# Four chained attention layers on one core: cross attention's first group of heads worked pair by pair

## What is computed

```python
def _mha(qx, kx, wq, bq, wk, bk, wv, bv, wo, bo, mask, bias):
    ...
    s = jnp.einsum('bhqd,bhkd->bhqk', q, k) / jnp.sqrt(jnp.asarray(DH, qx.dtype))
    ...
    a = jax.nn.softmax(s, axis=-1)
    o = jnp.einsum('bhqk,bhkd->bhqd', a, v).transpose(0, 2, 1, 3).reshape(Bq, Lq, D)
    return o @ wo + bo
...
sa = _mha(x, x, swq, sbq, swk, sbk, swv, sbv, swo, sbo, mask, bias)
x = _layernorm(x + sa, g1, be1)
ca = _mha(x, mem, cwq, cbq, cwk, cbk, cwv, cbv, cwo, cbo, None, None)
x = _layernorm(x + ca, g2, be2)
ff = jax.nn.gelu(x @ w1 + b1, approximate=False) @ w2 + b2
return _layernorm(x + ff, g3, be3)
```

## Time and profile before

| | us |
|---|---|
| median of three runs (lowest to highest) | 1641.1 (1638.26 to 1641.87) |
| the profiled execution's own time | 1641.36 |
| its span, first to last instruction | 1639.5 |
| mean granted TensorE clock | 0.953 |
| busy: PE, PE weight load | 1450.1 (88%), 723.9 (44%) |
| busy: DVE, ACT, POOL | 871.2 (53%), 727.2 (44%), 263.1 (16%) |

### The profile page before, as it was taken

How to read it: one execution, slowest core, us unless ns; L and a number is a source line. 1 busy time by engine, 2 the same in 40 slices (tenths; PEclk the granted TensorE clock), 3 DMA queues, 4 the chain that set the end, 5 groups by cost and what they waited for, 6 DMA issues and landing times.

```text
span 1639.5 us, 24133 instructions
## 1 busy us (share of the span) xinstructions
PE 1450.1 (88%) x8268; PEld 723.9 (44%) x8268; DVE 871.2 (53%) x2127; ACT 727.2 (44%) x1193; POOL 263.1 (16%) x129
## 2 busy tenths in 40 slices
PE   5999798888999889898899988888899998989886
PEld 2336455433533654542443464553253355455334
DVE  2662564485266355557346446446636635654761
ACT  0662253355266235427436425352725632724361
POOL 1004121301100413220110213211011040413001
PEclk9999798989999989998999998999999998999899
DMA  9001304313200220440310032214031005041210
GB/s 349 1 1 33 78 2 78 70 22 110 66 1 7 39 65 1 78 91 1 123 53 1 8 57 47 46 35 88 1 123 53 1 7 103 2 74 39 56 58 13
DMA packets 44776, 85.28 MB, mean 52 GB/s; under 512 B 10465, under 2 KB 27873, under 8 KB 44385
## 3 DMA queue, kind: packets, MB, share of 16 engines
q1 hardware_dynamic: 39600, 70.02, 16.9%
q10 hardware_dynamic: 5040, 13.54, 3.9%
HBM read 43.68 MB, written 2.10 MB: 28 GB/s over the span
## 4 chain that ended last, share of the span: by engine, by line
PE 63%; DVE 16%; issue 10%; ACT 5%; DMA 3%; ACTq 2%; POOL 0%; DVEq 0%; POOLq 0%
PE ring L1223 7%; PE obank L1233 7%; PE ring L1388 7%; PE ring L1179 7%; DVE nmax L1024 7%; PE ring L1213 6%; PE obank L1438 4%; PE ring L1379 3%; PE ring L1200 3%; PE ring L1289 3%; PE ring L1166 3%; ACT q_all L733 2%; ACTq L668 2%; PE ring L1137 2%; PE ring L1261 2%
## 5 line engine op out<-in xcount | busy, mean ns | idle before, releaser
L1024 DVE TENSOR_REDUCE nmax<-ring 128x2 f32<-128x1024 f32 (+1 forms) x192 | 218.3, 1175 | 47.7 <-PE ring L1388 31.8
L638 ACT ACTIVATE region_e<-region_d,nmin 128x512 f32<-128x512 f32 x256 | 182.6, 714 | 82.6 <-DVE nmin L877 80.9
L877 DVE CUSTOM_DVE_ANT_0 region_d<-ring,maskb 128x512 f32<-128x512 f32 x256 | 165.8, 686 | 92.7 <-issue 92.6
L746 ACT ACTIVATE region_e<-ring 128x1024 f32<-128x1024 f32 x192 | 183.5, 992 | 57.4 <-PE ring L1388 35.0
L733 ACT ACTIVATE q_all<-ring 2x1024 fp32r<-2x1024 bf16 x96 | 97.6, 1016 | 217.1 <-PE ring L1449 216.5
L563 POOL TENSOR_TENSOR nat_x<-nat_n,rows 128x1024 f32<-128x1024 f32 x16 | 37.6, 2350 | 632.6 <-DVE nat_n L922 463.1
L1020 DVE TENSOR_REDUCE nmax<-ring 128x4 f32<-128x512 f32 (+1 forms) x96 | 86.9, 912 | 96.1 <-PE ring L1379 94.5
L1379 PE MATMUL ring<-cbf 64*128 64x128 bf16 (+2 forms) x1280 | 136.5, 293 | 0.0
L1223 PE MATMUL ring<-region_q 64*128 64x512 f32 x512 | 126.9, 615 | 7.7 <-ACT region_q L627 5.4
L1233 PE MATMUL obank<-region_e,vs 128*64 128x512 f32 x512 | 124.0, 605 | 0.0
L1388 PE MATMUL ring<-k_tiles_a,q_all 64*128 64x512 f32 (+4 forms) x384 | 82.2, 472 | 29.1 <-DMA q_all<-q_parts 18.2
(11 more groups left out here) (175 smaller groups left out, 2163.9 us busy)
## 6 DMA issues: line engine op xcount, KB each, us to landing
k_tiles_a<-k_parts SPq DMA_DIRECT2D x144, 64.0 KB, 2.3
k_tiles_b<-k_parts SPq DMA_DIRECT2D x144, 64.0 KB, 2.3
q_all<-q_parts ACTq DMA_DIRECT2D x144, 64.0 KB, 3.4
q_all<-q_parts SPq DMA_DIRECT2D x144, 64.0 KB, 2.6
region_e<-in_w_f SPq DMA_DIRECT2D x8, 1024.0 KB, 5.6
wvo<-in_wv SPq DMA_DIRECT2D x5, 1024.0 KB, 5.5
wqk<-in_wq SPq DMA_DIRECT2D x4, 1024.0 KB, 9.6
wqk<-in_wk SPq DMA_DIRECT2D x4, 1024.0 KB, 11.5
```

The costliest lines, as they stand in the source:

```text
L638: ins = act.activation(e0[:, n % E0, h, :], sm0[:, n % 2, h, :], ACT.Exp, bias=nmin0[:, n, h:h + 1], scale=-1.0, accum_out=sum0[:, n, h:h ...
L746: act.activation(e16[:, n % 4, 2 * u:2 * u + 2, 0:nq], slot((a, "B", g, kt, u))[:, :, 0:nq], ACT.Exp)\
L877: ins = dve.tensor_tensor_reduce(out=sm0[:, n % 2, h, :], in0=slot(("S0", p, kt))[:, h, :], in1=maskb[:, :], scale=-1.0, scalar=3.0e38, op ...
L1024: dve.tensor_reduce(nmax[:, qt, 2 * u:2 * u + 2], slot(name)[:, :, 0:nk], AX.X, ALU.max, negate=True)\
```

## The change

In the cross attention (`a == FULL`) group 0 is handled pair by pair, by an order written out for it: the four passes A of pair 0, its maxima (`("M", 0, 0)`), two passes A of pair 1, pair 0's transposes (`("T", 0, 0)`), the other two passes, pair 1's maxima; then all four exponentials of pair 0 are placed ahead of those of pair 1, and group 1's passes A lie between them. The four passes A of group 2 that lay among group 0's last exponentials now follow `T` of group 1 in a row. `M` and `T` get a third entry: `None` for both pairs at once, as everywhere else, or the pair. The three keep-warm matmuls behind the last opening pass go in this attention. The list of jobs grows by one, to 244, so two pads are added.

```diff
+def opening_steps(a):
+
+    if a != FULL:
+        return [("A", 0, qt, u) for qt in range(NT) for u in pieces(a, "A", qt)] + [("M", 0, None)]
+    first, second = ([("A", 0, qt, u) for qt in range(NT)] for u in range(2))
+    return first + [("M", 0, 0)] + second[:2] + [("T", 0, 0)] + second[2:] + [("M", 0, 1)]
...
 def group_steps(a, g):
 
     steps = []
+    if g == 0 and a == FULL:
+        ones = [("A", 1, i, u) for i in range(NT) for u in range(2)]
+        return [("B", 0, 0, 0), ("B", 0, 1, 0), ones[0], ("T", 0, 1), ones[1], ("B", 0, 2, 0), ("B", 0, 3, 0), ones[2], ("B", 0, 0, 1),
+                ones[3], ("B", 0, 1, 1), ones[4], ("V", 0, 0), ("B", 0, 2, 1), ones[5], ("V", 0, 1), ("B", 0, 3, 1), ones[6], ones[7],
+                ("M", 1, None), ("T", 1, None), ("A", 2, 0, 0), ("A", 2, 0, 1), ("A", 2, 1, 0), ("A", 2, 1, 1)]
...
+def attention_steps(a):
+    return opening_steps(a) + [step for g in range(GROUPS) for step in group_steps(a, g)]
...
-                def maxima_rows(a, g):
-
-                    act.wait_ge(*filled_by((a, "T", g), b))
+                def maxima_rows(a, g, half):
+
+                    act.wait_ge(*filled_by((a, "T", g, half), b))
...
+                    own = slice(0, 2) if half is None else slice(half, half + 1)
                     for at in (32, 96):
-                        ins = act.activation(q_tiles[g][at:at + 2, :, :], turned[at:at + 2, :, :], ACT.Copy)
-                    ins.then_inc(*ends_drain((a, "T", g)))
+                        ins = act.activation(q_tiles[g][at:at + 2, own, :], turned[at:at + 2, own, :], ACT.Copy)
+                    ins.then_inc(*ends_drain((a, "T", g, half)))
...
-                def maxima_cols(a, g):
-
-                    high, low = (mcol[:, g % 2, :, :, i:i + 65:64] for i in (32, 33))
-                    top = nmax[:, :, :].rearrange("p t (u i) -> p t u i", u=2)
+                def maxima_cols(a, g, half):
+
+                    own = slice(0, 2) if half is None else slice(half, half + 1)
+                    high, low = (mcol[:, g % 2, :, own, i:i + 65:64] for i in (32, 33))
+                    top = nmax[:, :, :].rearrange("p t (u i) -> p t u i", u=2)[:, :, own, :]
...
-                    for u in range(2):
+                    for u in range(2) if half is None else (half,):
                         for t in range(NT):
                             ins = pe.transpose(turned[:, u * S + t * P:u * S + (t + 1) * P], mcol[:, g % 2, t, u, :], cb("ident", P))
...
-                    for qt in range(NT):
-                        for u in pieces(a, "A", qt):
-                            pass_a(a, 0, qt, u)
+                    for kind, *which in opening_steps(a):
+                        if kind == "A":
+                            pass_a(a, *which)
                             if a == FULL:
                                 keep_warm(2)
-                    keep_warm(3)
+                        if kind == "T":
+                            turn_maxima(a, *which)
+                    if a != FULL:
+                        keep_warm(3)
```

More of the change, by code:

```diff
@@ L128, in group_steps @@
     return steps
+def attention_steps(a):
+    return opening_steps(a) + [step for g in range(GROUPS) for step in group_steps(a, g)]
 def attention_jobs(a):
[L132 to L135, removed]
+    return [(a,) + step for step in attention_steps(a) if step[0] in "ABT"]
 def plan_jobs():
@@ L162 @@
 FIRST_LINKS = 6
-DVE_LINKS = 102
+DVE_LINKS = 103
 ACT_LINKS = 5
@@ L362, in ends_drain, with turns @@
             return drained[JOB[name] % SLOTS], 1
+        def turns(a, g, half, b):
+            return b * 13 + a * GROUPS + g + 1 + (1 if a == FULL and (g or half) else 0)
         def width(a, g_tile):
@@ L749, in attention @@
                 def attention(a):
[L750 to L758, removed]
+                    for kind, *which in attention_steps(a):
+                        if kind == "T":
+                            maxima_rows(a, *which)
+                        if kind == "B":
+                            if which == [0, 2 if a == CAUSAL else 3, 0]:
+                                for k in range(1, GROUPS):
+                                    act.wait_ge(k_stacked[k], (b * 3 + a + 1) * 96)
+                            exponentials(a, *which)
                 high_q(0)
@@ L1058, in attention @@
                 def attention(a):
-                    for qt in range(NT):
-                        for u in pieces(a, "A", qt):
[L1061 to L1070, removed]
+                    for kind, *which in attention_steps(a):
+                        if kind == "A":
+                            maxima(a, *which)
+                        if kind == "M":
+                            maxima_cols(a, *which)
+                        if kind == "H":
+                            head_out(a, *which)
                 drain_q_relu(("Q2",), "bq2")
@@ L1413, in pass_b @@
                     dst = start(name)
-                    if (kt, u) == (0, 0):
-                        pe.wait_ge(*drained_by((a, "T", g), b))
+                    if kt == 0 and u in (pieces(a, "B", 0) if a == FULL and g == 0 else (0,)):
+                        pe.wait_ge(*drained_by((a, "T", g, u if a == FULL and g == 0 else None), b))
                     q0, nq = width(a, kt)
@@ L1440, in values, with turn_maxima @@
                     ins.then_inc(pv_done, 1)
-                def turn_maxima(a, g):
-                    name = (a, "T", g)
+                def turn_maxima(a, g, half):
+                    name = (a, "T", g, half)
                     dst = start(name)
-                    pe.wait_ge(mcol_ready, b * 12 + a * GROUPS + g + 1)
+                    pe.wait_ge(mcol_ready, turns(a, g, half, b))
                     turned = dst[:, 0, :].bitcast(BF16)
-                    for u in range(2):
+                    for u in range(2) if half is None else (half,):
                         for t in range(NT):
```

14 lines of the change are left out of this document (7 added, 7 removed).

## The result

| | before | after |
|---|---|---|
| median of the runs made together (lowest to highest) | 1640.65 (1636.31 to 1641.87) | 1648.03 (1642.65 to 1649.27) |
| the profiled execution's own time | 1641.36 | 1649.16 |
| its span | 1639.5 | 1647.4 |
| mean granted TensorE clock | 0.953 | 0.950 |
| busy: PE, DVE, ACT | 1450.1, 871.2, 727.2 | 1443.3, 874.5, 727.2 |

The ratio is 1.0043, with an interval from 1.0025 to 1.0060: slower by about 7.1 us (4.1 to 9.8). The forecast was slower, 1652 in a range of 1639 to 1659. Sign and range are right; 7 stands where +11 was worked out. The lower PE busy time is no saving: the profile of the change holds 40 matmul records fewer, where its code has 12 matmuls fewer.

A forecast was written before the change was run, and what follows sets the result against it. Bound taken: turns of PE's three-slot PSUM ring, no engine full. 4 x (-1.3 + 1.9 + 2.1) + 0.5 = +11.3 on 1641.36 gives 1652.7, less 0.26 for the runs' median: 1652, range 1639 to 1659.

The forecast's parts named there:

- What bounds the kernel: Cross attention: no engine is full; PE's three PSUM slots wait for DVE or ACT reads, so time sums ring turns.
- Opening and first exponential: Start of cross attention: half transposes at 332.6, half copies 1.2 each, first exponential 4.5 earlier, ending as ACT idle time.
- Group 1's maxima late: Cross attention, group 1: columns of maxima ready 2.0 later, since its passes stand between twice as many exponentials.
- Order alone, -1.3: First pass to group 2's opening transposes (the mark): 34.4 against 35.73 a batch if the clock is never halved.
- First fall, +1.9: Half clock among group 1's maxima, lasting 6.83: their columns 1.9 later a batch, ends 0 and 3.8.
- Second fall, +2.1: Half clock over group 0's last values, after PE waits for group 1's columns: 2.1 a batch, ends 0 and 2.5.
- Boundary, +0.5: Between batches: added pads make PE wait 0.9 for DVE's read, 0.3 of it showing; +0.5 for three boundaries together.
- The clock did not hold: Rival, cross attention: no half clock in either place, total -4.7, 1636; chance 0.14.
- one fall only (+2.9): Rival, cross attention: half clock only at group 1's maxima, PE recovered before its wait; total +2.9, 1644; chance 0.20.
- a long fall of 10.24: Rival, group 1's maxima: half clock lasts 10.24, total +18.9 or 2.3 more, 1660 to 1662; chance 0.08.
- the boundary's cover: Between batches: DVE's return round its loop hides most of PE's 0.9 wait; without it the three cost 2.8.
- the exponentials did come early: Rival claimed the opposite: PE sits on the last opening passes, only 0.7 changes, under 3 in all, 1643; chance 0.03.

The follow-up runs named there:

- experiment 7: The change's split opening and half-wide copies, with the old kernel's interleaving behind them: 1637.42 against 1636.20 for the kernel before, ratio 1.0012.
- experiment 8: The change's split opening kept, group 1's passes A moved ahead of group 0's last two exponentials and all values: 1627.95 against 1636.20 before, ratio 0.9957.
- experiment 5: The change plus keep-warm matmuls in both places, among group 1's maxima and in the second wait: 1636.77 against 1638.92 for the kernel before, ratio 0.9989.
- experiment 4: The change plus 8 and 3 keep-warm matmuls in PE's second wait: 1643.67 against 1638.92 for the kernel before, ratio 1.0025.
- experiment 3: The kernel before with one pad ahead of the cross attention and two at a batch's end, 246 jobs: 1639.76 against 1636.20 before, ratio 1.0014.
- experiment 6: The kernel before plus 12 keep-warm matmuls in PE's waits among group 1's maxima: 1630.52 against 1636.20 for the kernel before, ratio 0.9959.
- experiment 2: The kernel before with three more pad jobs, all at a batch's end: 1649.15 against 1638.92 for the kernel before, ratio 1.0060.

## Why the prediction was right, and what was mis-sized

**What bounds the kernel**: right. A sum of turns of a three-slot ring; taking the same work in another order moved a batch's mark from 38.5 down to 35.7 (experiment 7) and 33.2 (experiment 8).

**Opening and first exponential**: right to 0.1 (5.71 for 5.8, 9.67 for 9.6, 1.19 for 1.2), and so is what it was worth, nothing: the 4.4 reappeared as ACT's wait of 3.20 and in the ring.

**Group 1's maxima late**: right, and this is the cause: with the passes moved forward again (experiments 7 and 8) the loss is gone. The prediction put the delay down to the exponentials; its own schedule also had the values in the way. The columns were scheduled at 24.5 and came at 24.88; over twelve batches of the change the transposes start at 24.3 to 25.0, mean 24.56.

**Order alone, -1.3**: not borne out as measured, and open as to size. With the clock held the mark came at 35.4, not 34.4, so -0.1 against 35.5. In the three batches of experiment 5 with that mark, the passes A of tile 2 start at 16.5 and 18.6, where the schedule had 15.9 and 17.6, and group 1's transposes at 23.6 for 22.7. Behind these both have 11.8 to the mark. The first 0.6 of the delay is the keep-warm matmul's in front of the pass, as shown there; carried on with the prediction's handovers and without the keep-warm matmuls, the transposes would start at about 22.7, an estimate from the rows of experiment 5 that no run shows. Above all, the comparison hid something: the old order was taken as it ran, with its falls. At full clock it has 33.4 to 33.6, so at equal clock the new order is a cost, of 1.9 as measured and of about 1.0 if the forecast's 34.4 holds.

**First fall, +1.9**: it came (6.83 in all twelve batches). At group 1's transposes it is worth 24.56 - 23.6 = +1.0 if experiment 5's delay is the order's, and 24.56 - 22.7 = +1.9 if it is the keep-warm matmuls'. The sum of this term and the order's is shown to be right there, and its split is not.

**Second fall, +2.1**: right in size. From those transposes to the mark it is 13.94 on average instead of 11.8. It lasted 6.83 or 10.24, and it went away in two batches of experiment 4, which put work into the wait.

The mark was thus forecast at 38.4 and is 38.5 over twelve batches. Against 35.5 (twenty batches of the old order) that is +3.0, four times +11.9, for a forecast of +10.8. Behind the mark before has a late fall more often (five of its twelve batches take 31.7 instead of 30.4, two of the change's), which leaves the attentions 10.6 longer.

**Boundary, +0.5**: too small. The prediction's own 0.3 a boundary already makes 0.8 for the three. The profile has 0.36 a boundary, so +1.1; the times of experiment 3 allow 0 to 4.4.

**The sum, +11.3**, is 4 above the measured 7.1. It is not the attentions that were priced too high: they lose 10.6. The prediction took the stretches outside them as fixed, and in the profiles they are 3.7 and 1.8 shorter. The second of these is chance, and of the first it is not known. So the attentions were forecast by their mechanism; that the run came out inside the range, and 4 under the sum, is nothing that the prediction explains.

**Rivals.** The clock did not hold; one fall only (+2.9) did not happen; a long fall of 10.24 did not come in the first place, but in three of twelve batches in the second; the boundary's cover gave way by a part only; the exponentials did come early. Of the page "TensorE: Matmul & The Clock Gate" of the Trainium skill, the section "A second HAM failure mode: psum-queue depth-cycling" fits what runs here show: both orders lose 2 to 3 a batch in waits of the ring, and filling the waits brings most of it back. "Loop structure matters more than you think", by which DVE's reading of PSUM leaves the warm state alone, does not hold here: in experiments 5 and 6 the falls went when PE had other work while it waited for DVE and ACT.

## What to carry to other kernels

When work is moved forward through a shared ring of buffers, ask what it pushes back. Here group 0's last exponentials and its values were free to wait and the next group's maxima were not: the same early start cost 0.4% with these first and gained 0.4% with the next group's passes ahead of them. Compare orders at equal clock before comparing them as they ran, and count what the matmuls that hold the clock cost themselves. See PE's waits as places behind which the clock fell here: with seven spare matmuls in them the best order went from 0.9957 to 0.9935, in another set of runs, with intervals that overlap.

## What the runs showed of the hardware that was not expected

- PE's jump back at the end of its loop takes 3.3 to 4.0, and is free only while matmuls are queued. With a wait ahead of it PE stood idle for 5.31, 3.98 of them the jump (experiment 2); with the same wait behind it, for 0.78.
- A 2 x 512 copy on ACT takes 0.60, as long as an exponential of 128 x 512: with 2 partitions or with 128 the time is the same.
- The half clock in a stretch is not fixed by the work in it: the same 1746 matmuls between two attentions had 17.1 to 27.3 us of it, and the stretch took 329.2 to 333.7.
